# A fused attention and expert block on one core: the DMAs of the maxima's rows move from ACT's queue to SP's, whose program is written by slots

## The reference, cut to what matters

```python
# x: (32, 128, 128), ctx: (32, 128, 128); 16 heads of 8
x = x + tanh(g_xattn) * cross_attention(layernorm(x), ctx, ctx)
x = x + tanh(g_ffn) * block(layernorm(x))
# cross_attention and the self attention inside block, for each sequence and head:
scores = einsum('bqhd,bkhd->bhqk', q, k)      # 128 x 128, block: causal
weights = softmax(scores, axis=-1)
out = einsum('bhqk,bkhd->bqhd', weights, v)
# block: rope, q/k/v projections, attention, layer norm, 2 of 8 experts, layer norm
```

## Time and profile before

| | us |
|---|---|
| median of 3 runs | 461.83 (461.24 to 461.96) |
| the profiled execution | 461.55 |
| its span, first to last instruction | 459.7 |
| PE busy | 399.5 |
| DVE busy | 375.3 |
| POOL busy | 320.1 |
| ACT busy | 278.0 |

### The profile page before, as it was taken

The page is one execution under the profiler, slowest core; times in us unless marked ns, Lnnn a source line. Parts: engine busy times, 40 slices in busy tenths (PEclk is TensorE's granted clock), DMA queues, the critical chain, the costliest instruction groups (busy, mean ns, idle before and its releaser), DMA issues.

```text
span 459.7 us, 17611 instructions
## 1 busy us (share of the span) xinstructions
PE 399.5 (87%) x6568; PEld 241.5 (53%) x6568; DVE 375.3 (82%) x1196; ACT 278.0 (60%) x705; POOL 320.1 (70%) x712
## 2 busy tenths in 40 slices
PE   0369888889878899999999999999879999999993
PEld 0235545445445566656666666666545555555542
DVE  6688999999998787878877877775167999999986
ACT  1126777776776666666666666666515666567562
POOL 4466677676698888878888788434743677777783
PEclk9999999999999999999999999999969999999997
DMA  6856696665444443334434443330000000000001
GB/s 163 198 141 167 178 202 168 167 177 131 123 118 116 108 118 98 94 101 108 108 102 115 113 109 96 100 91 14 2 0 1 1 24 24 11 25 18 19 24 46
DMA packets 88036, 42.75 MB, mean 93 GB/s; under 512 B 16000, under 2 KB 87824, under 8 KB 87952
## 3 DMA queue, kind: packets, MB, share of 16 engines
q1 hardware_dynamic: 76544, 38.61, 31.6%
q10 hardware_dynamic: 11408, 3.02, 2.9%
HBM read 5.69 MB, written 2.10 MB: 17 GB/s over the span
## 4 chain that ended last, share of the span: by engine, by line
PE 47%; ACT 5%; DVE 4%; issue 3%; POOL 0%; ACTq 0%; DVEq 0%; POOLq 0%
PE u_bank L445 7%; PE s_bank L804 7%; PE st_bank L804 6%; PE s_bank L383 4%; PE s_bank L396 3%; PE u_bank L822 3%; DVE r L619 2%; PE u_bank L792 2%; PE u_bank L820 2%; ACT z_x_t L871 2%; PE t_bank L375 2%; PE t_bank L369 2%; PE st_bank L396 2%; PE u_bank L458 2%; ACT part L506 1%
## 5 line engine op out<-in xcount | busy, mean ns | idle before, releaser
L638 DVE TENSOR_REDUCE nm<-s_bank 128x4 f32<-128x512 f32 x256 | 171.6, 683 | 37.8 <-PE s_bank L396 34.5
L528 ACT ACTIVATE pt<-st_bank 128x512 f32<-128x512 f32 x256 | 149.3, 601 | 77.1 <-PE u_bank L445 41.1
L396 PE MATMUL s_bank<-qk 64*64 64x128 bf16 (+1 forms) x1536 | 102.5, 221 | 12.2 <-DVE nm L638 6.0
L445 PE MATMUL u_bank<-pt,vaug 128*32 128x128 f32 x2048 | 109.5, 286 | 1.6
L396 PE MATMUL st_bank<-qk 64*64 64x128 bf16 (+1 forms) x1588 | 101.7, 218 | 0.0
L396 PEld LDWEIGHTS s_bank<-qk 64*64 64x64 bf16 (+1 forms) x1536 | 72.9, 104 | 36.2 <-issue 18.9
L396 PEld LDWEIGHTS st_bank<-qk 64*64 64x64 bf16 (+1 forms) x1588 | 72.1, 103 | 0.0
L445 PEld LDWEIGHTS u_bank<-pt,vaug 128*32 128x32 f32 x2048 | 40.8, 108 | 27.2 <-issue 3.8
L383 PE MATMUL s_bank<-mqk,idb 64*64 64x256 bf16 x256 | 38.3, 291 | 2.7 <-ACT pt L528 0.8
L383 PE MATMUL st_bank<-mkq,idb 64*64 64x256 bf16 x256 | 38.3, 293 | 0.1
L292 POOL TENSOR_TENSOR part<-r,part 128x512 bf16<-128x512 f32 x32 | 37.0, 1157 | 1.4
(11 more groups left out here) (129 smaller groups left out, 840.0 us busy)
## 6 DMA issues: line engine op xcount, KB each, us to landing
qk<-part SPq DMA_DIRECT2D x221, 128.0 KB, 2.8
x_all<-x SPq DMA_DIRECT2D x16, 128.0 KB, 2.7
qk<-qrow SPq DMA_DIRECT2D x32, 64.0 KB, 2.1
qk<-mts ACTq DMA_DIRECT2D x64, 32.0 KB, 2.4
c_all<-ctx_in SPq DMA_DIRECT2D x14, 128.0 KB, 2.8
out<-z_o SPq DMA_DIRECT2D x14, 128.0 KB, 1.8
ewt<-exp_t SPq DMA_DIRECT2D x1, 512.0 KB
qk<-part ACTq DMA_DIRECT2D x3, 128.0 KB, 2.6
```

The costliest lines, as they stand in the source:

```text
L396: ins = pe.matmul(to[outs, :], fixed[:, outs], moving, start=not masked, stop=True, skip_group_check=masked)
L445: ins = pe.matmul(u_bank[b][32 * j:32 * j + 32, r * P:(r + 1) * P], v, pt[m % 4][:, j, :], start=half == 0, stop=half == 1, skip_group_che ...
L528: act.activation(pt[m % 4][:, :, :].rearrange("k j q -> k (j q)"), st_bank[m % 2][:, :], ACT.Exp).then_inc(ex, 1)
L638: dve.tensor_reduce(nm[q % 2][:, first:first + HEADS], s_bank[n % 2][:, :].rearrange("q (j k) -> q j k", j=HEADS), AX_X, ALU.max, negate=T ...
```

## The change

ACT's copy of the maxima keeps its place, and the row's DMA behind it goes. SP gets a program over slots, like the other engines: at slot t = 1 the loads, at t = 2 a row, at t = 3 constants, at t = 5 the query rows and the first part of the stack of unit s + 2, at t = 6 a row and then the other six parts. The row waits on SP for ACT's copy. All DMAs keep their sizes and semaphores; the three middle parts of unit 0 stay on ACT.

```diff
         def sp_attention(sp):
-            for s in range(FIRST_SLOT // TILES, UNITS):
+            def max_row(q):
+                sp.wait_ge(mts_s, q + 1)
+                if q >= 2:
+                    sp.wait_ge(mrow[q % 2], 16 * (q // 2))
+                sp.dma_start(qk[(q // G) % RING][SLOTS:P:8, :, 0, (q % G) * P:(q % G + 1) * P],
+                             mts[q % 2][:, :]).then_inc(mrow[q % 2], 16)
+
+            def query_rows(u):
+                if u >= RING:
+                    sp.wait_ge(st, (u - RING + 1) * TILES)
+                sp.dma_start(qk[u % RING][SLOTS:P:8, :, 0, :], qrow[in_y(u)][:, :]).then_inc(stk[u % RING], 16)
+
+            for n in range(FIRST_SLOT, LAST_TILE + 3):
+                s, t = divmod(n, TILES)
                 u = s + 2
+                q = seq_at(n, 6)
+                if q is not None:
+                    max_row(q)
                 if 0 <= u < UNITS:
-                    if u >= RING:
-                        sp.wait_ge(st, (u - RING + 1) * TILES)
-                    sp.dma_start(qk[u % RING][SLOTS:P:8, :, 0, :], qrow[in_y(u)][:, :]).then_inc(stk[u % RING], 16)
-                    sp.wait_ge(h0_s, high_parts(u))
-                    stack_parts(sp, u, 0)
-                    if u >= 1:
-                        sp.wait_ge(h1_s, u + 1)
-                        stack_parts(sp, u, 1)
-                    sp.wait_ge(h2_s, u + 1)
-                    stack_parts(sp, u, 2)
-                if AHEAD <= s + 7 < GROUPS:
+                    if t == 5:
+                        query_rows(u)
+                        sp.wait_ge(h0_s, high_parts(u))
+                        stack_parts(sp, u, 0)
+                    if t == 6:
+                        if u >= 1:
+                            sp.wait_ge(h1_s, u + 1)
+                            stack_parts(sp, u, 1)
+                        sp.wait_ge(h2_s, u + 1)
+                        stack_parts(sp, u, 2)
+                if t == 1 and AHEAD <= s + 7 < GROUPS:
                     load_inputs(sp, s + 7)
-                if 0 <= s <= 8:
+                if t == 3 and 0 <= s <= 8:
                     later_constants(sp, 2 * s, 2 * s + 2)
-                elif 9 <= s <= 10:
+                elif t == 3 and 9 <= s <= 10:
                     later_constants(sp, 4 * s - 18, min(4 * s - 14, LATER))
...
                 act.activation(mts[q % 2][:, :], m_bank_b[:, 0:P], ACT.Copy).then_inc(mts_s, 1)
-                act.wait_ge(mts_s, q + 1)
-                act.dma_start(qk[(q // G) % RING][SLOTS:P:8, :, 0, (q % G) * P:(q % G + 1) * P],
-                              mts[q % 2][:, :]).then_inc(mrow[q % 2], 16)
```

## The result

| | before | after |
|---|---|---|
| median | 461.83 us (461.24 to 461.96) | 470.17 us (468.11 to 470.92) |
| ratio, 95% interval | | 1.0176 (1.0139 to 1.0213) |
| profiled execution | 461.55 us | 470.92 us |
| its span | 459.7 us | 469.1 us |

Slower by 8.3 us on the median and by 9.4 us in the profiled executions; the one of after stands at the upper end of its runs.

What follows compares the result with a forecast made beforehand. DVE bounds the x phase and PE the y phase, with SP as good as full; SP 8.2 us later, less 2.9 us slack, gives 5.3, less 0.7 is +4.6 us: 466.4 us, range 459.0 to 469.5.

Steps and rivals of the forecast that it cites:

- SP's sum: SP's issuing from unit 1's to unit 12's parts: rows, constants, loads and filled waits make it end 8.2 us later.
- The mechanism: x phase: SP, with 9.2 us of issuing against 8.38 us of computing per unit, sets the pace; chance 0.66.
- the slot order: SP's loads and constants stand ahead of the stack; at the start cost zero, 1.2 us without the hole.
- ACT's relief in the x phase: DVE's wait for ACT's high part ends: up to 0.36 us per unit, 5.0 us for 14 units.
- the price of a row: One row's DMA issue on SP: 0.58 us, bounds 0.41 and 0.66; 12.2 us for 21 rows.
- one rival: Half of SP's 8 us of issue stalls vanish among short rows: +0.6 us, 462.2 us; chance 0.14.
- slower by more: Rows land in 4.3 us and stalls fall on them, 0.1 us each: +8 us, 469.6; chance 0.08 above 469.5.
- SP's waits: SP's idle waits up to unit 12's parts, 3.7 + 0.9 = 4.6 us, are filled by the added issues.
- the slack: Unit 12's last part lands 2.9 us before PE's first product; this comes off SP's lateness, leaving tile 96 5.3 us late.
- the y phase at zero: y phase: ACT's relief gains zero, since PE's products release the exp at 204.35 us.
- PE's wait for DVE's remainder: y phase: 4.1 us in 14 units, the gain if taking zero there is wrong.
- The rival of the shared generator: SP already pays for ACT's issues, so SP isn't the bound: 456.5 us in full, 459 by half; faster case, chance 0.20.

Runs made afterwards that it cites:

- spare rows: Changed slot order on SP, ACT issuing the real rows as before, plus an unread 32 KB DMA on SP at each row's place: 473.6 us, ratio 1.0256.
- light kernels: Changed kernel, and kernel before, each without the last two of seven part DMAs in units 4 to 13: 458.27 us and 461.49 us.
- light after: Changed kernel with the last two of seven part DMAs left out of the stacks of units 4 to 13: 458.27 us, ratio 0.9928.
- no rows: Changed slot order on SP, with the row DMAs left out altogether, so maxima are not subtracted: 457.5 us, ratio 0.9909.
- the products at unit 12: Changed kernel with eight 128x128 f32 products before PE's wait for unit 12's stack, nowhere else: 467.64 us, ratio 1.0135.
- the order alone: Changed kernel's SP program by slots, but ACT issues the rows as before: 461.51 us, ratio 0.9994.
- both kernels with spare DMAs: Changed SP order, rows on ACT, plus an unread SP DMA at each row's place: 32 KB, 473.6 us; 256 bytes, 473.72 us.
- light before: Kernel before with the last two of seven part DMAs left out of the stacks of units 4 to 13: 461.49 us, ratio 0.9996.
- constants, spread: Changed kernel with the 25 constants issued by ACT, one at slots t = 0 and t = 4 of s = -1 to 11: 458.27 us, ratio 0.9925.
- the constants in ACT's first slots: Changed kernel with the 25 constants issued by ACT, two per slot in slots 0 to 12: 461.98 us, ratio 1.0006.

## Why the prediction was right in kind and too small

*What failed* is the size of SP's sum: SP was to be 8.2 us later at the end of unit 12's parts and was 12.0 us later, and 3.8 us of that is the price of the rows (12.2 us taken, 16.0 measured). To it came 1.0 us of a later landing, and behind it a half-clock stretch of 2.1 us that the prediction did not have. The parts of it follow, from the profiled executions.

*The mechanism was right.* SP was full, the rows made it the bound, PE came to wait for `part` at five of the units 5 to 12, and DVE behind PE. The spare rows show that SP's issue time alone does it, and the light kernels that it ends when SP gets room. That the slot order costs nothing was right too.

*ACT's relief in the x phase was right in kind, and half the size.* It was lost behind SP, as said, and DVE's wait for the high part is gone. But where SP has room, an x unit wins 0.20 us and not 0.36: light after, tiles 40 to 56, -1.6 to -2.0 in two units; no rows, tiles 64 to 96, -1.4 to -2.2 in four. There DVE waits for PE's scores instead: 3.5 us in 15 times with no rows, 1.2 us in 3 times before (44 to 140 us). And from tile 96 on the x units win nothing in any kernel (no rows, -2.2 to -1.9 at tile 128), so the 0.7 us that the sum took off for them did not come.

*The term that was mis-sized first: the price of a row.* SP's rows up to 126.8 us, ns min/median/max, and the parts of the same stretch with their landings:

```profile
L220 SPq DMA_DIRECT2D qk<-mts x21: 536/557/1949, 24.9 to 122.2; - x21
...
DMA to landing us min/median/max: 1.8/2.3/4.4
...
L212 SPq DMA_DIRECT2D qk<-part x78: 597/617/1557, 19.9 to 126.1; - x78
...
DMA to landing us min/median/max: 2.4/2.5/4.3
```

I took 0.54 us and a gap of 0.04. The median was near it, 0.557, but two of the 21 were stalled (1.95 and 1.45 us, at 50.21 and 60.48 us), and ahead of each row, with its two waits, there are 0.10 us (122.12 to 122.22). Added up from SP's timeline, the 21 issues take 13.9 us (11.7 at the median and 2.2 of stalls), and with 21 x 0.10 it is 16.0 us, 0.76 per row. The stalls didn't shrink, as one rival had it, nor become more: issues of over 0.8 us are 11 in both stretches, 8.2 us over the usual length before and 9.4 after. Some now fall on rows, as the rival "slower by more" had it; its slow landings of rows were wrong (median 2.3 us). The packets of the instruction queue are as many as the long issues, 11 in either stretch, and 9 of the 11 long issues before and 8 of 11 after have one that starts in them or within 0.3 us of them. That fits the prediction's argument that they come with the program; no run tested it.

*The second: SP's waits were not all filled.* The sum took off 4.6 us, and 3.3 us of idle time between issues went. 0.95 us is the new wait for ACT's first copy (23.91 to 24.86 us), too early in the program to be filled by anything behind it. And some of the 4.6 us was no hole: the query rows at 83.70 us are listed with a wait of 0.6 us, but start 0.04 us after the issue of `gbb`.

So SP's sum from the end of unit 1's parts to that of unit 12's, from its timelines:

| us | predicted | measured |
|---|---|---|
| rows | +12.2 | +16.0 |
| constants | +1.8 | +1.7 |
| loads | -1.2 | -1.8 |
| waits filled, and other gaps | -4.6 | -3.3 |
| parts, query rows | 0 | -0.6 |
| SP later at unit 12 by | +8.2 | +12.0 |

*The third: the slack.* The last part, issued at 126.1 us, let PE go at 130.05, 3.9 us later, where I had the median of 2.9. So 1.9 us of slack were used instead of 2.9, and tile 96 came 10.1 us late instead of 5.3. Why this landing took so long isn't shown. The x units from tile 64 to 96 took 9.9 us each, where 9.2 was expected.

*Not foreseen: the clock.* In PE's wait of 2.23 us, 0.6 us before its end, a half-clock stretch begins, 129.4 to 136.2 us. Unit 12 is the last one for which SP is the bound, so nothing hides that stretch, and it costs 2.1 us; the products at unit 12 take it away, and its price with it. The Trainium skill (TensorE: Matmul & The Clock Gate, HAM oscillation) tells of waits for DMAs, longer ones than this, that put PE back to its lower clock; the two sets of windows above agree, with a wait of 2.23 us.

*Wrong: the y phase at zero.* The y units went from 10.15 to 10.02 us (PE's tile starts 168 to 224, 71.03 and 70.12 us for seven units). The step that failed is the reading of the earlier trace rows: I looked at the exp at 204.35 us, the second behind the issue of slot 2, which PE's products release, and not at the first behind the issue of slot 6. ACT's and PE's timelines of before there:

```profile
228.01 0.28 ACT L535 ACTIVATE mts<-m_bank 128x128 bf16<-128x128 bf16 x1 [0.78 <-PE m_bank L453]
228.31 0.56 ACTq L537 DMA_DIRECT2D qk<-mts  x1
228.97 1.08 ACT L528 ACTIVATE pt<-st_bank 128x512 f32<-128x512 f32 x2 [0.69 <-PE u_bank L445]
```
```profile
229.17 0.42 PE L445 MATMUL u_bank<-pt,vaug 128*32 128x128 f32 x8
229.72 0.27 PE L383 MATMUL s_bank<-mqk,idb 64*64 64x256 bf16 x1
```

The first of the two exps starts 0.10 us behind the issue, not behind the products that the row names, and PE has a hole of 0.13 us before the first products of a unit, at 229.72. After, the exp starts 0.22 us behind the copy and PE goes on without the hole:

```profile
239.59 0.28 ACT L551 ACTIVATE mts<-m_bank 128x128 bf16<-128x128 bf16 x1 [0.78 <-PE m_bank L469]
240.09 0.60 ACT L544 ACTIVATE pt<-st_bank 128x512 f32<-128x512 f32 x1 [0.22 <-PE st_bank L412]
```
```profile
240.75 0.43 PE L461 MATMUL u_bank<-pt,vaug 128*32 128x128 f32 x8
241.17 0.27 PE L399 MATMUL s_bank<-mqk,idb 64*64 64x256 bf16 x1
```

The hole, some 0.1 us per unit, stands in every kernel in which ACT issues the rows of y (before, the order alone, both kernels with spare DMAs, light before) and in none of the others. PE's wait for DVE's remainder, to which I had tied a gain, stayed as it was.

*The rival of the shared generator fell.* With ACT's issues gone, a part's issue on SP kept its median of 617 ns; and before, from 20 to 160 us, the 29 parts issued while ACT issued a row have the same median as the 82 others. So SP had not been paying for ACT's issues, and moving them cost it their full price. The Trainium skill (Perfetto Trace Analysis, DMA Instruction — HWDGE) has one generator that is locked by one sequencer at a time, by which the move would be free; these runs don't agree. The Trainium skill (Perfetto Trace Analysis, DMA Optimizations) also advises to balance DMAs between the engines that can issue them, where issuing is the bottleneck. That held here: the 25 constants on ACT, spread, took the ratio from 1.0176 to 0.9925.

Added up for the profiled executions: +10.3 (SP) + 2.1 (clock) - 2.2 (y) - 0.8 = +9.4 us. The last term is behind the y tiles, where the half-clock stretch near 340 us lasts from 344.5 to 351.3 us instead of 332.1 to 342.3. The other profiles go with it, though no run changed it alone: behind tile 255 the four kernels in which it lasts 6.8 us win 0.7 to 1.0 us, the seven in which it lasts 10.2 or 10.3 us, as before, stand between -0.3 and +0.5, and the one with 13.7 us (constants, spread) loses 1.2. Open is also why some of these kernels scatter so much: after by 2.8 us over four runs, the spare rows by 5.2 over four, the constants in ACT's first slots by 5.8 over twelve, and before by 2.0 over 23.

## What to carry to other kernels

Count the issues of a DMA queue per unit of the loop before moving one to it: a queue with 8.0 us of issuing in a unit of 8.4 us is a full engine, though no page shows it as busy, and each DMA added to it costs the whole unit its issue, with stalls and the gap ahead of it (0.76 us here, where the median issue is 0.56). Look for what else can leave that queue (here 25 constants), or move the DMAs only in the phase where the queue has room: both gave 0.6 to 0.75% where the plain move lost 1.8%. And when an engine starts work 0.1 us after its own DMA issue, look at the issue first, whatever releaser the row names: here it was what ACT had waited for.

## What the runs showed of the hardware that was not expected

- The issue of a DMA on SP takes 0.54 us for 32 KB and 0.57 us for 256 bytes of one partition (medians of the two kernels with spare DMAs).
- SP's issues of parts have a median of 617 ns whether ACT issues at the same time or not.
- The granted clock of TensorE fell to 0.50 around waits of PE of 1.1 to 2.2 us in the middle of a phase in which PE was 86% busy before (after: from 64.6, 81.6, 102.1 and 129.4 us on). Not every such wait did it: with spare rows, waits of 1.62 and 1.14 us from 60.8 and 70.7 us on were followed by no half-clock stretch before 92.5 us. One half-clock stretch, with nothing to hide it, cost 2.1 us; eight products of 128x128 put into the wait took it away.
